# Four row buffers in the layer norm and two half-width QT buffers in the similarity stage

## The reference, cut to what matters

```python
xn = _layernorm(x, axis=-1)
s = _L0_attn_ref(xn, ...)          # the attention block, below
g = _silu(_L0_ffn_ref(xn, ...))    # two transformer layers with local attention and a feed-forward part
out = x + s * g

# _L0_attn_ref
normed = (x - mu) * rsqrt(var + LN_EPS) * ln_g + ln_b      # a second layer norm, on xn
h = silu(normed @ W_hidden + b_hidden); v, gate = split(h)
qk = silu(normed @ W_qk + b_qk)                            # 2048 x 2048
q = qk * os_gamma[0] + os_beta[0]
k = qk * os_gamma[1] + os_beta[1]
sim = einsum('bid,biD->bdD', q, k) / seq_len               # features by features, 2048 x 2048
attn = softmax(sim, axis=-1)
out = v * sum(attn, axis=-1)[:, None, :]
out = (out * gate) @ W_out + b_out + x
```

## Time and profile before

| | us |
|---|---|
| median of two timed runs | 4485.37 (4482.11 to 4488.63) |
| the profiled execution, its own time | 4479.04 |
| span of its slowest core, core 5 | 4477.5 |
| spans of the eight cores | 4457.3 to 4477.5 |
| mean granted TensorE clock of the cores | 0.771 to 0.801 |

### The profile page before, as it was taken

How to read it: one execution, slowest core, us unless ns; L and a number is a source line. 1 busy time by engine, 2 the same in 40 slices (tenths; PEclk the granted TensorE clock), 3 DMA queues, 4 the chain that set the end, 5 groups by cost and what they waited for, 6 DMA issues and landing times. The chain is left out here.

```text
span 4477.5 us, 36109 instructions; the slowest of 8 cores (4457.3 to 4477.5 us)
## 1 busy us (share of the span) xinstructions
PE 2964.0 (66%) x12624; PEld 1227.8 (27%) x12624; DVE 1406.4 (31%) x2349; ACT 849.9 (19%) x1314; POOL 176.8 (4%) x222
## 2 busy tenths in 40 slices
PE   1139568496935566665588998456666664989872
PEld 1113223243411222222133343112222221433332
DVE  2330532011134454444511111334444445111122
ACT  1222122232212122222111010221222212101110
POOL 0000000000000000000011111100000000111100
PEclk8569789798966765666699999666666676999985
DMA  4210000402330000000045555100000000555555
GB/s 83 64 43 0 1 0 1 75 1 48 132 104 19 19 1 1 1 1 1 9 62 62 61 70 58 28 19 10 1 1 0 1 10 12 69 63 60 67 98 169
DMA packets 227944, 170.34 MB, mean 38 GB/s; under 512 B 97573, under 2 KB 210360, under 8 KB 222648
## 3 DMA queue, kind: packets, MB, share of 16 engines
q0 software_dynamic: 195136, 94.42, 17.4%
q1 hardware_dynamic: 32632, 73.61, 5.0%
HBM read 237.26 MB, written 25.17 MB: 59 GB/s over the span
## 5 line engine op out<-in xcount | busy, mean ns | idle before, releaser
L1207 PE MATMUL pa<-N,W1B 128*128 128x512 bf16 x1408 | 338.8, 384 | 68.3 <-DMA W1B<-w1ag 68.2
L1311 PE MATMUL pS<-KP,QP 64*128 64x512 bf16 x448 | 206.5, 542 | 265.9 <-ACT PB L1339 216.4
L1339 ACT ACTIVATE PB<-pS,small 128x1024 bf16<-128x1024 f32 (+1 forms) x256 | 257.1, 1005 | 611.8 <-DVE small L1332 608.1
L1169 PE MATMUL px<-PROD,W2B 128*128 128x512 bf16 x1408 | 322.3, 386 | 48.2 <-DMA W2B<-w2cb 48.0
L1219 PE MATMUL pg<-N,W1B 128*128 128x512 bf16 x1408 | 335.3, 381 | 0.0
L1332 DVE TENSOR_REDUCE small<-pS 128x1 f32<-128x1024 f32 (+1 forms) x256 | 267.4, 1083 | 182.8 <-PE pS L1319 182.8
L1371 PE MATMUL pPT<-ident_bf,PB 128*128 128x128 bf16 x1792 | 205.1, 302 | 152.7 <-DVE PB L1354 152.7
L1231 DVE TENSOR_TENSOR PROD<-pa,GEB 128x1024 bf16<-128x1024 f32 x88 | 107.8, 1225 | 628.8 <-ACT GEB L1226 628.8
L604 PE MATMUL psim<-KF,QT 128*128 128x512 bf16 x1024 | 229.5, 388 | 111.8 <-DVE QT L592 111.8
L888 PE MATMUL pqkv<-ABF,WQKV 128*128 128x512 bf16 x768 | 204.8, 434 | 60.3 <-DVE ESC L835 42.8
L1371 PEld LDWEIGHTS pPT<-ident_bf,PB 128*128 128x128 bf16 x1792 | 187.2, 143 | 204.7 <-issue 204.0
(11 more groups left out here) (137 smaller groups left out, 2903.8 us busy)
## 6 DMA issues: line engine op xcount, KB each, us to landing
W1B<-w1ag POOLq DMA_DIRECT2D x88, 512.0 KB, 5.9
W2B<-w2cb POOLq DMA_DIRECT2D x32, 704.0 KB, 9.5
XT<-x SPq DMA_DIRECT2D x16, 512.0 KB, 4.9
xn_scr<-XNW SPq DMA_DIRECT2D x16, 512.0 KB, 3.4
WH<-W_hidden POOLq DMA_DIRECT2D x8, 1024.0 KB, 29.2
XNB<-xn_scr SPq DMA_DIRECT2D x8, 1024.0 KB, 7.0
s_scr<-SB SPq DMA_DIRECT2D x8, 1024.0 KB, 4.7
XF<-xn_scr SPq DMA_DIRECT2D x8, 1024.0 KB, 22.7
```

What stands on the lines that cost most here:

```text
L1169: e.matmul(px[:, pb, :], W2B[:, s2, k, :], PROD[:, k, cc * 512:(cc + 1) * 512], start=(k == 0), stop=False)
L1207: e.matmul(pa[:, mp, cc * 512:(cc + 1) * 512], W1B[:, sl, k, 0:128], self.N2[:, k, nh0 + cc * 512:nh0 + (cc + 1) * 512], start=(k == 0), s ...
L1311: e.matmul(pS[:, u, jc * 512:(jc + 1) * 512], QP[u * 64:(u + 1) * 64, hp, iv:iv + 128], KP[u * 64:(u + 1) * 64, hp, (jt0 * 128) + jc * 512 ...
L1339: p.task("scalar", lambda e, u=u, JW=JW, sc=sc, it=it: e.activation(PB[:, it % 2, u, 0:JW], pS[:, u, 0:JW], AF.Exp, bias=small[:, sc:sc + ...
```

## The change

In `phase0` XT, XNT, NTB, ST6 and MV get four buffers (`b = t % 4`), and the small columns for the reciprocal deviation move so that there are four of each. XNW and the two PSUM tensors keep two (`bp = t % 2`). The order of the tasks is as before.

In `attn_p2` the four groups of 512 columns become eight groups `dp` of 256 columns with two tiles `dt` each, and QT4 becomes QT2 with two buffers of half the width, of the same total size. The order of the tasks within a group is as before: build QT, then for each tile matmuls, maximum, bias, exponential, reciprocal, row sum.

```diff
-            XT = S.enter_context(nc.sbuf_tensor("XT", [128, 2, D], F32))
-            XNT = S.enter_context(nc.sbuf_tensor("XNT", [128, 2, D], F32))
-            NTB = S.enter_context(nc.sbuf_tensor("NTB", [128, 2, D], BF16))
+            XT = S.enter_context(nc.sbuf_tensor("XT", [128, 4, D], F32))
+            XNT = S.enter_context(nc.sbuf_tensor("XNT", [128, 4, D], F32))
+            NTB = S.enter_context(nc.sbuf_tensor("NTB", [128, 4, D], BF16))
             XNW = S.enter_context(nc.sbuf_tensor("XNW", [128, 2, DT, 128], F32))
-            ST6 = S.enter_context(nc.sbuf_tensor("ST6", [128, 2, 12], F32))
-            MV = S.enter_context(nc.sbuf_tensor("MV", [128, 2, 2], F32))
+            ST6 = S.enter_context(nc.sbuf_tensor("ST6", [128, 4, 12], F32))
+            MV = S.enter_context(nc.sbuf_tensor("MV", [128, 4, 2], F32))
...
             for t in range(NT):
-                b = t % 2
+                b = t % 4
+                bp = t % 2
                 p.dma("sync", XT[:, b, :], h["x"][t * 128:(t + 1) * 128, :],
                       writes=(f"XT{b}",), tag=f"p0.load{t}")
...
-                stats(XT[:, b, :], f"XT{b}", 12 + b, f"p0.s1_{t}", b)
+                stats(XT[:, b, :], f"XT{b}", 16 + b, f"p0.s1_{t}", b)
...
-                stats(XNT[:, b, :], f"XNT{b}", 14 + b, f"p0.s2_{t}", b)
+                stats(XNT[:, b, :], f"XNT{b}", 20 + b, f"p0.s2_{t}", b)
...
-                        mm = e.transpose(pbf[:, b, k * 128:(k + 1) * 128],
+                        mm = e.transpose(pbf[:, bp, k * 128:(k + 1) * 128],
                                          NTB[:, b, k * 128:(k + 1) * 128],
                                          self.ident_bf[:])
...
-                      XNW[:, b, :, :],
-                      reads=(f"XNW{b}",), writes=(f"xn_scr.{t}",),
+                      XNW[:, bp, :, :],
+                      reads=(f"XNW{bp}",), writes=(f"xn_scr.{t}",),
...
-            QT4 = S2.enter_context(nc.sbuf_tensor("QT4", [128, NT, 512], BF16))
+            QT2 = S2.enter_context(nc.sbuf_tensor("QT2", [128, 2, NT, 256], BF16))
...
-            for dtg in range(4):
+            for dp in range(8):
+                qp = dp % 2
                 for kt in range(NT):
-                    p.task("vector", lambda e, dtg=dtg, kt=kt: e.tensor_tensor(
-                        QT4[:, kt, :], QK[:, kt, dtg * 512:(dtg + 1) * 512],
-                        GBC[:, 0, dtg * 512:(dtg + 1) * 512], op=ALU.mult),
-                        reads=(f"QK{kt}.{dtg}",) + gbc_res,
-                        writes=(f"QT4.{kt}",), tag=f"p2.qm{dtg}.{kt}")
...
+                    p.task("vector", lambda e, dp=dp, kt=kt, qp=qp: e.tensor_tensor(
+                        QT2[:, qp, kt, :], QK[:, kt, dp * 256:(dp + 1) * 256],
+                        GBC[:, 0, dp * 256:(dp + 1) * 256], op=ALU.mult),
+                        reads=(f"QK{kt}.{dp // 2}",) + gbc_res,
+                        writes=(f"QT2{qp}.{kt}",), tag=f"p2.qm{dp}.{kt}")
+                    p.task("vector", lambda e, dp=dp, kt=kt, qp=qp: e.tensor_tensor(
+                        QT2[:, qp, kt, :], QT2[:, qp, kt, :],
+                        GBC[:, 1, dp * 256:(dp + 1) * 256], op=ALU.add),
+                        reads=(f"QT2{qp}.{kt}",), writes=(f"QT2{qp}.{kt}",),
+                        tag=f"p2.qa{dp}.{kt}")
-                qt_res = tuple(f"QT4.{kt}" for kt in range(NT))
-                for dt in range(dtg * 4, dtg * 4 + 4):
+                qt_res = tuple(f"QT2{qp}.{kt}" for kt in range(NT))
+                for dt in range(dp * 2, dp * 2 + 2):
                     pb = dt % 2
-                    dl = (dt % 4) * 128
-                    def simmm(e, dt=dt, pb=pb, dl=dl):
+                    dl = (dt % 2) * 128
+                    def simmm(e, dt=dt, pb=pb, dl=dl, qp=qp):
                         for c in range(4):
                             for kt in range(NT):
                                 mm = e.matmul(
                                     psim[:, pb, c * 512:(c + 1) * 512],
-                                    QT4[:, kt, dl:dl + 128],
+                                    QT2[:, qp, kt, dl:dl + 128],
```

More of the change, by code:

```diff
@@ L442, in stats, with tp_n @@
                         reads=(f"lnv{b}",), writes=(f"rstd{rstd_col}",), tag=tagp + ".ex")
[L444 removed]
+                stats(XT[:, b, :], f"XT{b}", 16 + b, f"p0.s1_{t}", b)
                 p.task("vector", lambda e, b=b: e.tensor_scalar(
[L446 removed]
+                    XNT[:, b, :], XT[:, b, :], MV[:, b, 0:1], small[:, 16 + b:17 + b],
                     op0=ALU.subtract, op1=ALU.mult),
[L448 removed]
+                    reads=(f"XT{b}", f"MV{b}", f"rstd{16 + b}"),
                     writes=(f"XNT{b}",), tag=f"p0.xn{t}")
[L450 removed]
+                stats(XNT[:, b, :], f"XNT{b}", 20 + b, f"p0.s2_{t}", b)
                 p.task("vector", lambda e, b=b: e.tensor_scalar(
[L452 removed]
+                    NTB[:, b, :], XNT[:, b, :], MV[:, b, 0:1], small[:, 20 + b:21 + b],
                     op0=ALU.subtract, op1=ALU.mult),
[L454 removed]
+                    reads=(f"XNT{b}", f"MV{b}", f"rstd{20 + b}"),
                     writes=(f"NTB{b}",), tag=f"p0.nt{t}")
[L457 removed]
+                def tp_n(e, b=b, bp=bp):
                     for k in range(DT):
[L459 removed]
+                        mm = e.transpose(pbf[:, bp, k * 128:(k + 1) * 128],
                                          NTB[:, b, k * 128:(k + 1) * 128],
@@ L463, in phase0, with ev_n @@
                 p.task("tensor", tp_n, reads=(f"NTB{b}", "identity_bf"),
-                       writes=(f"pbf{b}",), tag=f"p0.tpn{t}")
-                def ev_n(e, t=t, b=b):
+                       writes=(f"pbf{bp}",), tag=f"p0.tpn{t}")
+                def ev_n(e, t=t, bp=bp):
                     for k in range(DT):
@@ L469, in ev_n @@
                             ABF[:, k, t * 128:(t + 1) * 128],
-                            pbf[:, b, k * 128:(k + 1) * 128],
+                            pbf[:, bp, k * 128:(k + 1) * 128],
                             AF.Identity, bias=self.lnb_sb[:, k:k + 1],
@@ L473, in ev_n, with tp_x @@
                     return mm
-                p.task("scalar", ev_n, reads=(f"pbf{b}", "lng_t", "lnb_t"),
+                p.task("scalar", ev_n, reads=(f"pbf{bp}", "lng_t", "lnb_t"),
                        writes=(f"ABF.{t}",), tag=f"p0.evn{t}")
-                def tp_x(e, b=b):
+                def tp_x(e, b=b, bp=bp):
                     for k in range(DT):
-                        mm = e.transpose(pxf[:, b, k * 128:(k + 1) * 128],
+                        mm = e.transpose(pxf[:, bp, k * 128:(k + 1) * 128],
                                          XNT[:, b, k * 128:(k + 1) * 128],
@@ L483, in phase0, with ev_x @@
                 p.task("tensor", tp_x, reads=(f"XNT{b}", "identity_f32"),
-                       writes=(f"pxf{b}",), tag=f"p0.tpx{t}")
-                def ev_x(e, t=t, b=b):
+                       writes=(f"pxf{bp}",), tag=f"p0.tpx{t}")
+                def ev_x(e, t=t, b=b, bp=bp):
                     for k in range(DT):
-                        mm = e.tensor_copy(XNW[:, b, k, :],
-                                           pxf[:, b, k * 128:(k + 1) * 128])
-                    return mm
-                p.task("vector", ev_x, reads=(f"pxf{b}",),
-                       writes=(f"XNW{b}",), tag=f"p0.evx{t}")
+                        mm = e.tensor_copy(XNW[:, bp, k, :],
+                                           pxf[:, bp, k * 128:(k + 1) * 128])
+                    return mm
+                p.task("vector", ev_x, reads=(f"pxf{bp}",),
+                       writes=(f"XNW{bp}",), tag=f"p0.evx{t}")
                 p.dma("sync",
                       self.xn_scr.rearrange("k p n -> p k n")[:, :, t * 128:(t + 1) * 128],
-                      XNW[:, b, :, :],
-                      reads=(f"XNW{b}",), writes=(f"xn_scr.{t}",),
+                      XNW[:, bp, :, :],
+                      reads=(f"XNW{bp}",), writes=(f"xn_scr.{t}",),
                       tag=f"p0.spill{t}")
```

5 lines of the change are left out of this document (removed).

## The result

The changed kernel takes 1.0100 times as long as the kernel before (95% interval 1.0079 to 1.0122), some 45 us more. The profiled execution took 4523.87 us against 4479.04, +44.8.

What follows compares the result with a forecast made beforehand. TensorE, busy two thirds of the span, was taken to stand still while VectorE builds QT. Stalls +55.2 us, first build -4.3, layer norm 0: +50.9 us on 4479.04, plus 6.3 to the timed median, gives 4536 us (range 4515 to 4570).

Steps and rivals of the forecast that it cites:

- The second buffer stays unused, VectorE's order decides: Similarity stage: each QT build stands behind the previous group's maximum and reciprocal, so all 7 group changes stay full stalls.
- Seven stalls of 16.99 us instead of three of 21.25: Similarity group changes: 7.31 us fixed plus a 9.68 us build each; stalls total 118.9 us instead of 63.8, +55.2 us.
- The line through two widths: QT build instructions: times at 512 and 2048 columns extended to 256 give 287 and 293 ns, 9.68 us a build.
- The clock part of a stall stays: TensorE in similarity stalls: granted clock still falls to 0.50 and stays there 3 to 6 us after each restart.
- Rival 4: Similarity restarts: low clock lasting 8 to 11 us costs 5.5 us more per stall, slower by over 2%; chance 0.02.
- Layer norm: 0 us: First stage: four buffers change nothing because each load queues behind the previous spill on SyncE; 0 us, 16 waits remain.
- Behind the similarity stage the kernel is moved later as a whole; I add 0 for it.: All stages after similarity: shifted later by the same amount on each core, their own duration unchanged; 0 us.

Runs made afterwards that it cites:

- (3): Only the similarity part of the change (256-column groups, layer norm as before), with one QT buffer instead of two: ratio 1.0084 to the kernel before, against 1.0085 with two.
- (4): Only the similarity part of the change, with the next QT build put ahead of the second tile's reciprocal: ratio 1.0044 to the kernel before, 1.0085 without the move.
- (5): Only the similarity part of the change, with the next group's QT build put ahead of the current group's two tiles: ratio 0.9819 to the kernel before.
- 128 columns: Similarity stage in sixteen groups of 128 columns, one tile each, two QT buffers, task order as in the changed kernel: ratio 1.0324 to the kernel before.
- (6): Kernel before with the four layer norm buffers and the load of tile t+2 put at the head of tile t: ratio 0.9799 to the kernel before.
- pad 192: Kernel before plus 12 one-column memsets per similarity tile on VectorE, 192 in all, between bias and reciprocal: ratio 0.9969 to the kernel before.
- norm only: Only the layer norm part of the change (four buffers), similarity stage as in the kernel before: ratio 0.9995 to it.

## Why the prediction was right, and where it was off

- *The second buffer stays unused, VectorE's order decides.* Right, and shown three ways: taking the buffer away costs nothing (3), moving one instruction out of the way gives 2.4 us a stall (4), moving the build ahead removes all seven (5).
- *Seven stalls of 16.99 us instead of three of 21.25.* Right: idle time before the matmuls 154.8 us (154 forecast), mean stall 16.9 us, stage +51.4 us (+50.9 forecast). The line through two widths held at 256 and at 128 columns, to 1 ns. The table of VectorE: DVE Perf Modes (Trainium skill, section on the TRN2 errata), 58 cycles plus half the columns, gives 194 ns at 256 columns; measured are 286 and 293.
- *The clock part of a stall stays.* Right: 0.50 through the stall read and for 4.5 us behind it (3 to 6 forecast).
- *Rival 4, a low clock of 8 to 11 us costs 5.5 us more.* This sum is wrong, though nothing hung on it. At 0.50 a stretch of work takes about twice its time (6 matmuls in 2 us against 11), so 5.5 us more need 11 us more of low clock on top of the 3 to 5.5 us in the rows, some 14 to 16 us.
- *Layer norm: 0 us.* Right (0.9995 alone, 16 waits as before), and for the reason given: with the order changed the 86 us come free (6).
- *"Behind the similarity stage the kernel is moved later as a whole; I add 0 for it."* This term was mis-sized. The two local attention stages gave back 9.9 and 11.5 us in the median of the cores. Of that, 6 us arrived in the total: +51 in the stage, +45 over all. On the slowest cores it was 3680.0 us from the last maximum of the similarity stage to the end before (797.53 to 4477.5) and 3670.0 after (852.29 to 4522.3), where the forecast had the same distance; up to that maximum it was 54.8 us more, where the forecast had 50.9. That the total came within 6 us of the forecast is therefore in part luck: the slowest core had 10 us more in the last stretch of the kernel, which hid part of the miss. The forecast stood on the same instructions taking the same time behind the stage; their number and form did stay, but the matmuls among them ran at another granted clock (the median score matmul of core 1 takes 603 ns in before and 582 in pad 192).

Shown is that the place of VectorE's instructions selects the family of patterns in which local attention runs, with 192 and 256 added by memsets, in both directions and with both group widths, and what it is worth: the medians of the two stages sum to 1296.6 to 1306.0 us at a shift of 0 or 256 and to 1281.9 to 1292.6 at 192 or 576. A single stage of a single core overlaps (at shift 0 norm only had cores from 638 to 655 us in the first, at 192 pad 192 had 635 to 654 in the second). Shown too is that the place moves the points at which VectorE is late by some 0.35 us, beside a packet of its program. Runtime: NRT & Kernel Launch of the Trainium skill says in its section on instruction fetch mechanics that an engine's instruction memory is refilled in blocks of 256 instructions and that crossing into the next block is mostly hidden. The packets on VectorE's queue here hold 128, and the measurement decides: in blocks of 256 the shifts of 192 and 576 would be different places, in blocks of 128 they are the same, and the two kernels run alike. Mostly hidden agrees with the packet at 19.5 us, and not with the one at 58.7. Not shown is the last step, how single delays of 0.35 us, which all these kernels have, turn into blocks that are 3 us longer at a lower clock; that they push TensorE's bursts from one pattern into another is a reading.

## What to carry to other kernels

A second buffer buys nothing while the producer's instructions stand, on their own engine or queue, behind an instruction that waits for the consumer: look in the timeline for an engine that idles in front of one instruction with ready work right behind it, and move the work, not the buffer count. If the order stays, smaller pieces make it worse, since each change pays the fixed chain (here 7.3 us) again and each instruction its fixed part (here some 154 to 160 ns). When two versions differ by less than about 0.4%, compare the untouched stages too, or pad the engine's instruction count back by whole packets of its instruction queue (here 128; 256 was tried) before believing in the difference.

## What was not expected of the hardware

Adding 192 VectorE instructions that do nothing made the kernel 0.3% faster (0.9969, 0.9953 to 0.9986), 256 did not (1.0004). Of six blocks of equal work read in local attention four took about 38 us at a granted clock of 0.68 to 0.73 and two 41 us at 0.58 to 0.62, and which of them are slow follows the place of the instructions in VectorE's program. That program arrives in packets of 8192 bytes, 128 instructions each, and beside a packet one instruction can be 0.35 us late.
